# An LSTM step in two halves: two instead of three units of the second half's products ahead of the wait for the second half's h

## The chip, the cores and the metric

The kernel runs on one core of a Trainium2 chip. The time is the device time of one execution in microseconds; the figure for a kernel is the median of several executions. Traces come from one further execution, taken by the hardware profiler.

## What is computed

The input x is 4 sequences of 1024 steps with 512 features. Four layers are applied one after the other, each with a residual: a sparsifying mask, an LSTM, a gated scan, and a second LSTM. The change is in the code of the LSTMs, which run 1024 steps each, 2048 together:

```python
xW = einsum('ntd,dg->ntg', x, Wx) + b
def step(carry, xw_t):
    prev_h, prev_c = carry
    a = xw_t + prev_h @ Wh
    i = sigmoid(a[:, :512]); f = sigmoid(a[:, 512:1024])
    o = sigmoid(a[:, 1024:1536]); g = tanh(a[:, 1536:])
    next_c = f * prev_c + i * g
    next_h = o * tanh(next_c)
    return ((next_h, next_c), next_h)
```

h and c have 4 rows (the batch) of 512 values. Every step needs the h of the step before, so the steps cannot overlap each other.

## The kernel before, in words

`program` (L884) runs five stages in turn: `load_and_sparsify`, `lstm` with names that begin with p_, `gated_scan`, `lstm` with names that begin with q_, and `store`. The LSTM keeps features on the partitions. The 512 hidden values are four chunks k of 128; the 2048 gate columns are split in two **halves** called first (A) and second (B): each half has all four gates of two of the chunks of h. So the first half makes chunks 0 and 1 of the new h, and the second half makes chunks 2 and 3, but both halves need all four chunks of the old h.

**A unit of products** is one call of `h_product` (L406 to L412): the four matmuls j = 0 to 3 of one half, one chunk k of h and one part of the weights. The weights are two float16 parts (high and low), so that a half needs 4 chunks x 2 parts = 8 units a step: 4 with chunks 0 and 1 (`of_first`) and 4 with chunks 2 and 3 (`of_second`). Each of the four matmuls writes its own 32 partitions of the half's PSUM bank (tile PA or PB), with 256 columns; the four run beside each other in the array. h itself (tile H) is stored as a high and a low float16 part.

**The order on PE** (TensorE) is written out by hand in a loop of 128 rounds of 8 steps (v = 0, 1 and u = 0 to 3):

```python
in_between, rest = of_first[:BETWEEN], of_first[BETWEEN:]   # L417
...
pe.wait_ge(s["h_a"], now)                                   # L443
for k, part in of_first:
    h_product(first, v, u, k, part)
for k, part in in_between:
    h_product(second, v, u, k, part)
pe.wait_ge(s["h_b"], now)                                   # L448
for k, part in of_second:
    last = h_product(first, v, u, k, part)
last.then_inc(s["gates_a"], 1)                              # L451
for k, part in rest + of_second:
    last = h_product(second, v, u, k, part)
last.then_inc(s["gates_b"], 1)                              # L454
```

After it come four units of products of x for later steps (L459, matmuls of line L402), and in the steps with u = 0 two bias products (L456 to L458, line L397). So a step is: wait for h_a (chunks 0 and 1 are there), 4 units of A, some units of B, wait for h_b (chunks 2 and 3), 4 units of A, signal gates_a, the remaining units of B, signal gates_b.

**The order on DVE** (VectorE, L626 to L661) is also fixed. Here "first" and "second" are the halves. Wait for gates_a; transpose the first half's gates out of PA (L633, L634, both at line L597); add the two parts of h's products, `both_parts` (L602), signal pre_a; wait for gates_b (L637) and transpose the second half's i, f and g out of PB (L638); wait for g_a and `multiply` the first half (L605); wait for that transpose and run `both_parts` on the second half together with the first's o gate (L642), signal pre_b; `new_c` of the first half (L608); transpose and add the second's o gate; `whole_h`, `high_h` of the first (L615, L618); `multiply` the second; `low_h` of the first (L623), signal h_a; `new_c` of the second; wait for tc_b; `whole_h`, `high_h`, `low_h` of the second, signal h_b.

**ACT** (ScalarE, L494 to L508) answers in between: tanh of the first half's gates (L497, signals g_a), sigmoid of its o (L500), tanh of its c (L502), then the same for the second half (L503, L506, L508). **POOL** (GpSimd, L379 to L389) works every fourth step: it adds h onto x (L389) when the fourth h_b has come, and splits the x of a later group of steps (L355, L356, L359).

Of the kernel before, what the change touches and what calls it, by code (L numbers as in the profile page):

```python
# [31 lines left out]
XCOLS = T * B  # L32
V = 4
VB = V * B
BETWEEN = 3
SUMS = NC * B
PREP = 6
XTAIL = 2 * UB
# [212 lines left out]
def lstm(nc, m, tag, x_all, weights, wh, b, wh_there, also_load=()):  # L251
# [7 lines left out]
    with ExitStack() as ctx:  # L259
# [132 lines left out]
        def _(pe):  # L392
# [23 lines left out]
            of_second = [(k, part) for k in second.ks for part in range(2)]  # L416
            in_between, rest = of_first[:BETWEEN], of_first[BETWEEN:]  # L417

# [504 lines left out]
```

## Time and profile before

| | us |
|---|---|
| median of 3 runs | 7890.69 (7889.62 to 7891.22) |
| the profiled execution, its own time | 7896.71 |
| its span in the trace | 7894.5 |
| PE matmul busy | 5371.6 (68%) |
| DVE busy | 5546.4 (70%) |
| ACT busy | 2263.5 (29%) |
| POOL busy | 843.5 (11%) |

The span is the time from the first to the last instruction of the profiled execution. A busy share is the time in which at least one instruction of the engine was under way. In the rows, "PE" is the matmul side of TensorE and "PEld" its weight loads; L409 is the matmul inside `h_product`. The start times of two instructions on the same engine can be nearer to each other than one lasts, since the engines are pipelined. An entry x16 is sixteen matmuls merged, that is four units.

### The profile page before, as it was taken

What the parts mean: (1) busy time and instruction counts of PE and PEld (TensorE: products, weight loads), DVE (VectorE), ACT (ScalarE), POOL (GpSimd) and SP (SyncE); (2) the same over time, 40 slices, a digit from 0 to 9 for tenths busy, and PEclk for the clock granted to TensorE, in tenths of its full rate; (3) what the DMA queues carried; (4) which work ended last, traced back from release to release, by engine and by line L of the source; (5) the groups of instructions that cost most, each with busy time, mean ns of one, the idle gap of its engine ahead of it and who ended that gap; (6) DMA issues with size and microseconds to landing.
All of it is one profiled execution on the core that took longest, in us unless ns stands there. A gap on an engine that the chain in (4) does not pass through costs nothing. (4 is left out here: it accounts for less than half of the span.)

```text
span 7894.5 us, 402402 instructions
## 1 busy us (share of the span) xinstructions
PE 5371.6 (68%) x169280; PEld 4152.5 (53%) x169280; DVE 5546.4 (70%) x35379; ACT 2263.5 (29%) x12741; POOL 843.5 (11%) x2143
## 2 busy tenths in 40 slices
PE   1577777666777777666983776667777776667776
PEld 0455555555555555555431555555555555555555
DVE  7766777776666677776678777776666777766666
ACT  4322222222222222222354222222222222222222
POOL 5100000000000000000013000000000000000000
PEclk5899999999999999999996999999999999999999
DMA  2000000000000000000001000000000000000001
GB/s 85 17 0 0 0 0 0 0 0 0 0 0 0 0 0 0 0 0 0 0 0 43 0 0 0 0 0 0 0 0 0 0 0 0 0 0 0 0 0 43
DMA packets 32261, 37.24 MB, mean 5 GB/s; under 512 B 6112, under 2 KB 22496, under 8 KB 32224
## 3 DMA queue, kind: packets, MB, share of 16 engines
q1 hardware_dynamic: 32224, 36.76, 1.4%
q8 instruction: 21, 0.34, 0.0%
q14 instruction: 16, 0.13, 0.0%
HBM read 28.34 MB, written 8.39 MB: 5 GB/s over the span
## 5 line engine op out<-in xcount | busy, mean ns | idle before, releaser
L409 PE MATMUL q_PA<-scratch,q_H 128*8 128x256 f16 (+1 forms) x32768 | 1258.3, 274 | 1058.9 <-DVE q_H L623 1058.9
L409 PE MATMUL p_PA<-scratch,p_H 128*8 128x256 f16 (+1 forms) x32768 | 1257.5, 274 | 1059.0 <-DVE p_H L623 1059.0
L409 PEld LDWEIGHTS q_PA<-scratch,q_H 128*8 128x8 f16 (+1 forms) x32768 | 647.8, 90 | 1487.4 <-DVE q_H L623 1346.8
L409 PEld LDWEIGHTS p_PA<-scratch,p_H 128*8 128x8 f16 (+1 forms) x32768 | 647.3, 90 | 1487.4 <-DVE p_H L623 1346.8
L409 PE MATMUL q_PB<-scratch,q_H 128*8 128x256 f16 (+1 forms) x32768 | 1250.1, 273 | 0.0
L409 PE MATMUL p_PB<-scratch,p_H 128*8 128x256 f16 (+1 forms) x32768 | 1249.6, 273 | 0.0
L597 DVE STREAM_TRANSPOSE q_GT<-q_PA 128x192 f32<-128x192 f32 (+1 forms) x2048 | 526.3, 295 | 744.7 <-PE q_PA L409 744.7
L597 DVE STREAM_TRANSPOSE p_GT<-p_PA 128x192 f32<-128x192 f32 (+1 forms) x2048 | 526.3, 295 | 743.8 <-PE p_PA L409 743.8
L409 PEld LDWEIGHTS q_PB<-scratch,q_H 128*8 128x8 f16 (+1 forms) x32768 | 834.7, 92 | 59.9
L409 PEld LDWEIGHTS p_PB<-scratch,p_H 128*8 128x8 f16 (+1 forms) x32768 | 834.1, 92 | 60.2
L497 ACT ACTIVATE q_GBA<-q_PREA 128x24 f32<-128x24 f32 x1024 | 194.8, 190 | 1898.0 <-DVE q_PREA L602 1898.0
L497 ACT ACTIVATE p_GBA<-p_PREA 128x24 f32<-128x24 f32 x1024 | 195.0, 190 | 1896.6 <-DVE p_PREA L602 1896.6
L597 DVE STREAM_TRANSPOSE q_GT<-q_PB 128x192 f32<-128x192 f32 (+1 forms) x2048 | 639.5, 312 | 0.0
L597 DVE STREAM_TRANSPOSE p_GT<-p_PB 128x192 f32<-128x192 f32 (+1 forms) x2048 | 639.4, 312 | 0.0
L389 POOL TENSOR_TENSOR xb<-xb,q_HH 128x64 f32 x256 | 81.9, 320 | 3164.3 <-DVE q_H L623 3164.3
L389 POOL TENSOR_TENSOR xa<-xa,p_HH 128x64 f32 x256 | 81.7, 319 | 3163.7 <-DVE p_H L623 3163.7
L602 DVE TENSOR_TENSOR q_PREA<-q_GT 128x24 f32<-128x24 f32 (+1 forms) x2048 | 368.2, 180 | 34.9
L602 DVE TENSOR_TENSOR p_PREA<-p_GT 128x24 f32<-128x24 f32 (+1 forms) x2048 | 368.0, 180 | 34.9
L738 PE MATMUL g_z<-xa,scratch 128*128 128x512 f32 x768 | 352.2, 620 | 48.2 <-DVE scratch L790 45.6
L623 DVE SCALAR_TENSOR_TENSOR q_H<-q_HH,q_H 128x8 f16<-128x8 f32 x2048 | 342.1, 167 | 35.5
L623 DVE SCALAR_TENSOR_TENSOR p_H<-p_HH,p_H 128x8 f16<-128x8 f32 x2048 | 341.9, 167 | 35.4
L615 DVE TENSOR_TENSOR p_HH<-p_SIGOB,p_TCB 128x8 f32<-128x8 f32 x1024 | 166.2, 162 | 251.9 <-ACT p_TCB L508 251.9
(220 smaller groups left out, 9260.0 us busy)
## 6 DMA issues: line engine op xcount, KB each, us to landing
scratch<-in_x_dram SPq DMA_DIRECT2D x8, 1024.0 KB, 5.4
out_dram<-xa SPq DMA_DIRECT2D x16, 512.0 KB, 6.0
xb<-in_L_cond_Wx_dram SPq DMA_DIRECT2D x8, 384.0 KB, 6.4
xb<-in_L_cond_Wh_dram SPq DMA_DIRECT2D x8, 384.0 KB, 6.2
xa<-in_L_cond_Wx_dram SPq DMA_DIRECT2D x8, 384.0 KB, 5.9
xa<-in_L_cond_Wh_dram SPq DMA_DIRECT2D x8, 384.0 KB, 6.0
xb<-in_L_cond_Wx_dram SPq DMA_DIRECT2D x8, 128.0 KB, 6.7
xb<-in_L_cond_Wh_dram SPq DMA_DIRECT2D x8, 128.0 KB, 6.5
```

The lines of the kernel that those rows point to most:

```text
L389: nc.gpsimd.tensor_tensor(here, here, HH[:, v].rearrange("p u (c b) -> p c u b", b=B), ALU.add).then_inc(s["xadd"], 1)
L409: last = nc.tensor.matmul(half.banks[buf][Q * j:Q * j + rows, 0:GA * Q], H[:, u, k, 0:rows], w16[:, part, k, j, half_cols(half)], start=False,
L497: nc.scalar.activation(first.tanhs, first.pre_gif.rearrange("p (n m) -> p n m", n=3), ACT.Tanh, scale=half_scale).then_inc(s["g_a"], 1)
L597: return nc.vector.transpose(GT[:, lo:hi, :].rearrange("p g n -> p (g n)"), half.banks[v][:, (lo - half.at) * Q:(hi - half.at) * Q])
L602: return nc.vector.tensor_tensor(by_unit(dst), GT[:, lo:hi, at:at + B], GT[:, lo:hi, at + B:at + 2 * B], ALU.add)
L615: return nc.vector.tensor_tensor(HH[:, v, u, half.cols], half.sig_o[:], half.tanh_c, ALU.mult)
L623: return nc.vector.scalar_tensor_tensor(nxt[:, :, B:2 * B], by_unit(HH[:, v, u, half.cols]), H_SCALE, nxt[:, :, 0:B], ALU.mult, ALU.subtract)
L738: last = nc.tensor.matmul(banks[w * 2 + n % 2][:], wt[:, w, k, c * P:(c + 1) * P], m.xa[:, k, blk * TBB:(blk + 1) * TBB], start=(k == 0), ...
```

## The change

The constant `BETWEEN` goes from 3 to 2. With it `in_between` is the first two of `of_first` and `rest` the last two: the unit (k = 1, high part) of the second half's products, four matmuls, is issued behind the wait for h_b and the four units of the first half, instead of ahead of them. The order of the sums within each bank, all instructions and all signals stay.

```diff
 VB = V * B
-BETWEEN = 3
+BETWEEN = 2
 SUMS = NC * B
```

## Rows read from the trace of the kernel before

**Rows 1.** The page: span, engines, a group of weight loads (busy, mean ns, idle)

```profile
span 7894.5 us, 402402 instructions
...
PE 5371.6 (68%) x169280; PEld 4152.5 (53%) x169280; DVE 5546.4 (70%) x35379; ACT 2263.5 (29%) x12741; POOL 843.5 (11%) x2143
...
L409 PEld LDWEIGHTS q_PA<-scratch,q_H 128*8 128x8 f16 (+1 forms) x32768 | 647.8, 90 | 1487.4 <-DVE q_H L623 1346.8
```

**Rows 2.** One stretch: busy PE, PEld, DVE, ACT, POOL, then granted clock, DMA

```profile
400.00:3700.00 3300.00, 2311.37 (x78312) 1841.12 (x78304) 2309.27 (x16235) 874.77 (x5730) 289.77 (x952) 1.00 0.00 0
```

**Rows 3.** Waits, 400 to 3700 us: total us, times, longest us

```profile
PE p_PA L409 <- DVE p_H L623: 988.6, 955, 1.1
DVE p_GT L597 <- PE p_PA L409: 690.3, 955, 0.7
```

**Rows 4.** Timeline of one step: start us, us, engine, line, operation

```profile
2004.55 0.61 PE L409 MATMUL p_PA<-scratch,p_H 128*16 128x256 f16 x16 [0.86 <-DVE p_H L623]
...
2004.99 0.50 PE L409 MATMUL p_PB<-scratch,p_H 128*16 128x256 f16 x12
2005.10 0.17 DVE L623 SCALAR_TENSOR_TENSOR p_H<-p_HH,p_H 128x8 f16<-128x8 f32 x1
...
2005.32 0.61 PE L409 MATMUL p_PA<-scratch,p_H 128*16 128x256 f16 x16
...
2005.76 0.72 PE L409 MATMUL p_PB<-scratch,p_H 128*16 128x256 f16 x20
2005.98 0.51 DVE L597 STREAM_TRANSPOSE p_GT<-p_PA 128x192 f32<-128x192 f32 x2 [0.72 <-PE p_PA L409]
...
2006.30 0.61 PE L402 MATMUL p_PA<-xb,p_XH 128*32 128x256 f16 x16
2006.42 0.17 DVE L602 TENSOR_TENSOR p_PREA<-p_GT 128x24 f32<-128x24 f32 x1
2006.53 0.38 DVE L597 STREAM_TRANSPOSE p_GT<-p_PB 128x192 f32<-128x192 f32 x1
2006.63 0.19 ACT L497 ACTIVATE p_GBA<-p_PREA 128x24 f32<-128x24 f32 x1 [1.83 <-DVE p_PREA L602]
2006.85 0.18 DVE L605 SCALAR_TENSOR_TENSOR p_PRA<-p_GBA 128x16 f32<-128x16 f32 x1
2006.95 0.20 DVE L602 TENSOR_TENSOR p_PREB<-p_GT 128x32 f32<-128x32 f32 x1
...
2007.77 0.17 DVE L623 SCALAR_TENSOR_TENSOR p_H<-p_HH,p_H 128x8 f16<-128x8 f32 x1
...
2007.99 0.62 PE L409 MATMUL p_PA<-scratch,p_H 128*24 128x256 f16 x16 [1.07 <-DVE p_H L623]
```

**Rows 5.** Timeline of the first step of a round

```profile
1905.48 0.72 PE L409 MATMUL p_PB<-scratch,p_H 128*8 128x256 f16 x20
...
1906.05 0.32 POOL L356 TENSOR_TENSOR p_XH<-xa,p_SXB 128x64 f16<-128x64 f32 x1
...
1906.15 0.27 DVE L602 TENSOR_TENSOR p_PREA<-p_GT 128x24 f32<-128x24 f32 x1
...
1906.33 0.37 DVE L597 STREAM_TRANSPOSE p_GT<-p_PB 128x192 f32<-128x192 f32 x1
...
1906.51 0.32 POOL L359 TENSOR_TENSOR p_XH<-p_XC,p_XH 128x64 f16<-128x64 f32 x1
1906.67 0.20 DVE L605 SCALAR_TENSOR_TENSOR p_PRA<-p_GBA 128x16 f32<-128x16 f32 x1
1906.79 0.19 DVE L602 TENSOR_TENSOR p_PREB<-p_GT 128x32 f32<-128x32 f32 x1
```

**Rows 6.** Line L497: duration min/median/max, first and last start

```profile
L497 ACT ACTIVATE p_GBA<-p_PREA x1024: 190/190/193, 247.6 to 3782.9; 128x24 f32<-128x24 f32 x171
```

**Rows 7.** Timeline of PE where the second LSTM's loop begins, at the lower clock

```profile
4325.76 1.09 PE L409 MATMUL q_PA<-scratch,q_H 128*8 128x256 f16 x16
4326.61 0.67 PE L409 MATMUL q_PB<-scratch,q_H 128*8 128x256 f16 x8
```


## The prediction, made before the changed kernel was run

> **What bounds the kernel now.** I read the page first. Neither PE (68% of the span) nor DVE (70%) is full [rows 1], and the split by stages says why: through the LSTM loop PE is busy 2311 of 3300 us and DVE 2309, with TensorE granted its full clock, 2.4 GHz [rows 2]. Two engines at 70% each that take turns are a chain, not a shortage of either. The waits show the turns: in 955 steps PE waits 988.6 us for h from DVE (1.04 a step), and DVE waits 690.3 us for PE's gates (0.72 a step) [rows 3]. DMA is idle there. So the time is the length of one step's chain, 2048 times: 3.44 us a step (2004.55 to 2007.99) [rows 4], or 3.456 as the mean over a whole LSTM, (3782.9 - 247.6) / 1023 [rows 6].
>
> The reader should follow one step in the timeline [rows 4]. PE starts the 4 units of A at 4.55 (leaving out 2000), 3 units of B at 4.99, the other 4 units of A at 5.32, the remaining 5 units of B at 5.76, the products of x at 6.30. From 5.32 to 6.30 nine units go by in 0.98, so **a unit costs 0.109 us**. DVE transposes A at 5.98 and B at 6.53; each starts 0.05 after the last matmul of its half ends (5.32 + 0.61 = 5.93; 5.76 + 0.72 = 6.48). So B's transpose is held by gates_b and by nothing on DVE.
>
> **What sets the second start of A.** The second half's h is written at 5.10 + 0.17 = 5.27, and A's second batch starts 0.05 later, at 5.32. The same 0.05 stands between the first half's h (7.77 + 0.17 = 7.94) and the next first batch (7.99), where PE is certainly waiting [rows 4]. The three units of B also end their issue at 4.99 + 3 x 0.109 = 5.32. Both meet on the same hundredth: three units just fill the wait, and the wait is not shorter than they are.
>
> **The change part by part.** Nothing is removed or added; one unit of B (four matmuls) moves behind the wait and behind the second batch of A. No queue but PE's has another order.
>
> 1. *Ahead of the wait:* PE is through with B at 4.99 + 0.22 = 5.21, and waits till 5.32. Gain: none, since h_b doesn't come sooner. The 0.11 becomes idle PE. Cost of a drained engine at the restart: no row shows this very place drained. One bound is a whole weight load with nothing to hide it, 0.09 us (a mean of 90 ns) [rows 1]; the other is nothing, or 0.01 gained if the queue held it. The nearest row is the first batch, same shapes, after a real wait: 4 units in 4.99 - 4.55 = 0.44, and the second batch takes 5.76 - 5.32 = 0.44 as well [rows 4]. I take 0, with 0.01 either way, and keep the bare load as a rival.
> 2. *A's second batch* starts and ends as before: gates_a and DVE's transposes at 5.98, `both_parts` at 6.42, ACT's tanh at 6.63 don't move.
> 3. *B behind it* is six units, not five: its last matmul ends at 6.59, and DVE's transpose moves from 6.53 to 6.64, **+0.109**. In DVE's fixed queue the first half's `multiply` stands behind this wait, though its own input is there: tanh ends at 6.63 + 0.19 = 6.82, and it starts 0.03 later, at 6.85 [rows 4]. It can't start before the transpose has gone through, at most 0.32 after its start (6.53 to 6.85): 6.96 at the latest. `both_parts` of the second half needs the whole transpose: 6.91 and 0.04 on, 6.95 now; then 7.02 and 0.04 on, 7.06, again +0.11. Slack there is 0.
> 4. *What follows* down to the first half's h (6.95 to 7.77) is DVE back to back with ACT's answers between, each started by these two, so it moves whole. Step: 0.77 (4.55 to 5.32) + 10 units 1.09 + 0.23 (last unit's start plus one to DVE: 6.53 - 6.30) + 1.46 (6.53 to 7.99) = 3.55 against 3.44.
> 5. *Hidden, cost 0:* the products of x start 0.11 later; PE was idle 0.86 to 1.07 before the next h_a, and that h_a is later too. If that cover were gone it would be 0.11 again. POOL and ACT wait for the same h and gates and have no shorter path.
>
> **The first step of a round** (one in eight, 256 in all) is different [rows 5] (times leave out 1900). `both_parts` takes 0.27 there instead of 0.17, and ends at 6.42, 0.05 after POOL's L356 (6.05 + 0.32 = 6.37). So B's transpose starts at 6.33, while PE had it ready for 5.48 + 0.72 + 0.05 = 6.25. A gates_b later by 0.109 gives 6.36: +0.03. `multiply` is then at 6.36 + 0.32 = 6.68 against 6.67, and `both_parts` at 6.36 + 0.37 + 0.04 = 6.77 against 6.79 now, where it stands 0.12 behind the `multiply`. The stall that is paid there today covers nearly all of the unit: 0 to 0.03, I take 0.005; the far bound is the full 0.109.
>
> The row shows that stall; the Trainium skill has a rule for it (page "SBUF — State Buffer", section "Who interferes with whom"): a DVE instruction with two SBUF inputs and a GpSimd one that reads SBUF exclude each other, and the later blocks fully. The trace agrees with it twice, `both_parts` ending 0.05 after L356 and `multiply` (6.67 + 0.20 = 6.87) 0.04 after L359 (6.51 + 0.32 = 6.83). By it the end of this `multiply` is fixed by POOL and the first step would cost 0, not 0.005: a total smaller by 1 us.
>
> **Sum:** 1792 x 0.109 = 195.3, and 256 x 0.005 = 1.3: **+196.6 us**. The profiled execution took 7896.71 (span 7894.5 and 2.2 around it), so it would take 8093.3; the median of the runs is 6.0 below the profiled one, so I forecast 7890.7 + 196.6 = **8087 us**, 2.5% slower. Its own range: the hundredths of the rows are worth 0.005 x 1792 = 9 us either way, 8078 to 8096.
>
> **Rivals.**
> - *The first step pays in full* (slower by more): the stall on POOL moves along with the unit instead of covering it. 2048 x 0.109 = 223 us: 8114. For it: the stall's causes are only seen from outside. Against: both ends at POOL's instruction. 12%.
> - *Part of the unit is absorbed*: DVE finds 0.01 or so (6.82 + 0.03 is what holds `multiply` now, not the transpose). 1792 x 0.096 = 172: 8063. Against it: `both_parts` has no slack. 5%.
> - *Not slower, the other side:* the second batch of A is held by PE's own queue, not by h_b. Then one unit fewer ahead of it starts it 0.11 sooner, at 5.21, gates_a comes 0.11 sooner, gates_b when it does now, and seven steps in eight stay (B's transpose and `both_parts` are held by gates_b); in the first of a round `both_parts` may get ahead of POOL and save up to 0.11: 256 x 0.11 = 28 us. So 7863 to 7891. It decides if h_b is there before 5.32 by more than a hundredth or two. For it: three units end on that same hundredth. Against: the 0.05 after h's write, equal to that of the batch which surely waits. 5% (2 faster by over 0.2%, 3 within). Within it stands the case that the change has no effect since the wait has none.
> - *The restart of the drained engine costs a bare weight load:* 2048 x 0.09 = 184 us more, 8271. Against it the two equal 0.44. 2%.
> - *The clock:* PE's idle time is cut into two pieces a step. Where PE began the second LSTM's loop at half clock, 1.2 GHz, after the idle preparation, four units took 4326.61 - 4325.76 = 0.85, 0.2125 each [rows 7]. If the loop ran so, 16 units in a row would be 3.40 instead of 0.77 + 1.09, +1.54 on 3.55 and 2048 steps: about 11,240 us. Against: the loop already has a pause of about 1 us in each step and was granted the full clock through 3300 us [rows 2]. 1%. The Trainium skill (page "TensorE: Matmul & The Clock Gate", section "A second HAM failure mode: psum-queue depth-cycling") says that frequent short idles between groups of matmuls can make the clock swing between its two levels; the rows with such idles show no swing, and hang no more than this 1% on it.
>
> **How the numbers follow.** Forecast 75%, first step in full 12%, absorbed 5%, not slower 5%, bare load 2%, clock 1%. The range 8063 to 8115 takes in the forecast's own range and the next two cases; what is left out is about 1 in 10. About 0.2%, 16 us, is what a measurement of this kernel can tell from no change. Faster 0.02, same 0.03, slower 0.95.
>
> **What the changed profile would show.** Twelve matmuls between the batches become eight, twenty become twenty-four. A pause of 0.11 before the second batch of A, put down to DVE L623, so PE's waits of that kind double in number. The second batch 0.77 after the first, as now; A's transpose 0.66 after that; B's transpose 0.66 behind A's, now 0.55, and `multiply` 0.32 behind it, with ACT done 0.1 before. Steps of 3.55; in the first of a round a `both_parts` of 0.27 still, and hardly a longer step. L497 spans 1023 x 3.552 = 3634 us in each LSTM. I am wrong if the second batch starts before 0.77, or if `both_parts` follows gates_b by less than now.

## The result and the profile after

The changed kernel takes **8065.75 us** (median, 8062.28 to 8067.49) against 7890.95 for the kernel before (7889.62 to 7895.05): a ratio of 1.0219, with an interval of 1.0206 to 1.0232. That is 175 us slower. The forecast was 8087, 197 us slower, in a range of 8063 to 8115. Its own narrower range, 8078 to 8096, does not hold the result.

The page of the changed kernel, with the span and the engines' busy time:

```profile
span 8060.2 us, 402402 instructions
...
PE 5590.9 (69%) x169280; PEld 4151.8 (52%) x169280; DVE 5635.7 (70%) x35379; ACT 2248.5 (28%) x12741; POOL 846.6 (11%) x2143
```

The number of instructions is the same. The span of this one execution is 165.7 us longer than that of [rows 1]; it lies at the low end of its runs, while the traced execution of before lay above its own. So the traces differ by 166 us and the medians by 175.

One stretch of the first LSTM's loop, as in [rows 2] (PE, PEld, DVE, ACT, POOL, granted clock, DMA):

```profile
400.00:3700.00 3300.00, 2357.80 (x76512) 1798.41 (x76512) 2296.79 (x15862) 847.71 (x5598) 286.28 (x936) 1.00 0.00 0
```

The clock is still granted in full. Fewer instructions go by in the same 3300 us, on every engine. The waits of the same stretch, beside [rows 3]:

```profile
PEld p_PA L409 <- DVE p_H L623: 1408.9, 1866, 1.3
PE p_PA L409 <- DVE p_H L623: 942.4, 933, 1.1
```

There are now 933 steps in the stretch, not 955. PE's weight loads wait for h twice a step (1866 times; once a step, 955 times, before), and its matmuls are still shown as waiting once, since the modelled end of the last matmul of B covers the new gap. Now one step in the timeline, to be laid beside [rows 4]:

```profile
1946.54 0.61 PE L409 MATMUL p_PA<-scratch,p_H 128*16 128x256 f16 x16 [0.86 <-DVE p_H L623]
...
1946.98 0.39 PE L409 MATMUL p_PB<-scratch,p_H 128*16 128x256 f16 x8
1947.09 0.17 DVE L623 SCALAR_TENSOR_TENSOR p_H<-p_HH,p_H 128x8 f16<-128x8 f32 x1
1947.31 0.33 PEld L409 LDWEIGHTS p_PA<-scratch,p_H 128*16 128x16 f16 x16 [0.22 <-DVE p_H L623]
1947.31 0.61 PE L409 MATMUL p_PA<-scratch,p_H 128*16 128x256 f16 x16
...
1947.75 0.83 PE L409 MATMUL p_PB<-scratch,p_H 128*16 128x256 f16 x24
1947.97 0.51 DVE L597 STREAM_TRANSPOSE p_GT<-p_PA 128x192 f32<-128x192 f32 x2 [0.72 <-PE p_PA L409]
...
1948.62 0.19 ACT L497 ACTIVATE p_GBA<-p_PREA 128x24 f32<-128x24 f32 x1 [1.83 <-DVE p_PREA L602]
1948.63 0.38 DVE L597 STREAM_TRANSPOSE p_GT<-p_PB 128x192 f32<-128x192 f32 x1
1948.94 0.13 DVE L605 SCALAR_TENSOR_TENSOR p_PRA<-p_GBA 128x16 f32<-128x16 f32 x1
1949.05 0.20 DVE L602 TENSOR_TENSOR p_PREB<-p_GT 128x32 f32<-128x32 f32 x1
1949.16 0.16 DVE L608 SCALAR_TENSOR_TENSOR p_GBA<-p_PRA 128x8 f32<-128x8 f32 x1
1949.23 0.24 DVE L597 STREAM_TRANSPOSE p_GT<-p_PB 128x64 f32<-128x64 f32 x1
...
1949.86 0.17 DVE L623 SCALAR_TENSOR_TENSOR p_H<-p_HH,p_H 128x8 f16<-128x8 f32 x1
...
1950.08 0.62 PE L409 MATMUL p_PA<-scratch,p_H 128*24 128x256 f16 x16 [1.06 <-DVE p_H L623]
```

With times that leave out 1900: A's first batch 46.54, two units of B at 46.98 (x8), and a weight load that waited 0.22 for DVE L623. The second batch starts at 47.31, 0.77 after the first and 0.05 after the second half's h (47.09 + 0.17), exactly as before. Six units of B (x24) follow it. A's transpose is at 47.97, 0.66 behind the batch as before; ACT's tanh too is where it was, 0.65 behind the transpose. But B's transpose stands 0.66 behind A's, not 0.55, and `multiply` at 48.94, when its input has been there since 48.62 + 0.19 = 48.81. From 46.54 to 50.08 the step takes 3.54, not 3.44.

Behind `both_parts` the two kernels also differ. In the step of [rows 4], `both_parts` (6.95) is followed by:

```profile
2007.06 0.17 DVE L608 SCALAR_TENSOR_TENSOR p_GBA<-p_PRA 128x8 f32<-128x8 f32 x1
2007.14 0.24 DVE L597 STREAM_TRANSPOSE p_GT<-p_PB 128x64 f32<-128x64 f32 x1
```

From `new_c` to the transpose behind it, it was 0.08 before (7.06 to 7.14) and is 0.07 after (49.16 to 49.23).

The first step of a round, beside [rows 5]:

```profile
1944.43 0.52 DVE L597 STREAM_TRANSPOSE p_GT<-p_PA 128x192 f32<-128x192 f32 x2 [0.72 <-PE p_PA L409]
...
1944.76 0.32 POOL L356 TENSOR_TENSOR p_XH<-xa,p_SXB 128x64 f16<-128x64 f32 x1
...
1944.86 0.26 DVE L602 TENSOR_TENSOR p_PREA<-p_GT 128x24 f32<-128x24 f32 x1
...
1945.08 0.38 DVE L597 STREAM_TRANSPOSE p_GT<-p_PB 128x192 f32<-128x192 f32 x1
...
1945.39 0.20 DVE L605 SCALAR_TENSOR_TENSOR p_PRA<-p_GBA 128x16 f32<-128x16 f32 x1
1945.51 0.19 DVE L602 TENSOR_TENSOR p_PREB<-p_GT 128x32 f32<-128x32 f32 x1
1945.62 0.17 DVE L608 SCALAR_TENSOR_TENSOR p_GBA<-p_PRA 128x8 f32<-128x8 f32 x1
1945.70 0.24 DVE L597 STREAM_TRANSPOSE p_GT<-p_PB 128x64 f32<-128x64 f32 x1
```

`both_parts` (44.86) is as long as before and ends at 45.12, 0.04 after POOL's L356. B's transpose starts at 45.08, 0.65 behind A's (44.43), but `multiply` (45.39) comes 0.63 behind POOL's L356 and 0.12 ahead of the second `both_parts` (45.51), against 0.62 and 0.12 before. This step got no longer. Over a whole LSTM, as in [rows 6]:

```profile
L497 ACT ACTIVATE p_GBA<-p_PREA x1024: 191/191/193, 247.3 to 3865.8; 128x24 f32<-128x24 f32 x171
```

(3865.8 - 247.3) / 1023 = 3.537 us a step, 0.081 more than 3.456; times 2048 that is the 166 us.

### The profile page after: what moved, and what is told of

It is laid out like the page before. It is cut to its first block and busy times, and to the rows that moved or that the text cites. A ratio compares the mean times of both kernels' runs of the same rounds, so it can differ in the third digit from the quotient of the medians.

```text
span 8060.2 us, 402402 instructions
## 1 busy us (share of the span) xinstructions
PE 5590.9 (69%) x169280; PEld 4151.8 (52%) x169280; DVE 5635.7 (70%) x35379; ACT 2248.5 (28%) x12741; POOL 846.6 (11%) x2143
## 5 line engine op out<-in xcount | busy, mean ns | idle before, releaser
L497 ACT ACTIVATE q_GBA<-q_PREA 128x24 f32<-128x24 f32 x1024 | 196.2, 192 | 1895.7 <-DVE q_PREA L602 1895.7
L497 ACT ACTIVATE p_GBA<-p_PREA 128x24 f32<-128x24 f32 x1024 | 196.2, 192 | 1894.1 <-DVE p_PREA L602 1894.1
L623 DVE SCALAR_TENSOR_TENSOR q_H<-q_HH,q_H 128x8 f16<-128x8 f32 x2048 | 341.4, 167 | 35.4
L623 DVE SCALAR_TENSOR_TENSOR p_H<-p_HH,p_H 128x8 f16<-128x8 f32 x2048 | 341.3, 167 | 35.4
L615 DVE TENSOR_TENSOR q_HH<-q_SIGOB,q_TCB 128x8 f32<-128x8 f32 x1024 | 166.4, 162 | 251.6 <-ACT q_TCB L508 251.6
```

Source lines behind the costliest of these rows:

```text
L497: nc.scalar.activation(first.tanhs, first.pre_gif.rearrange("p (n m) -> p n m", n=3), ACT.Tanh, scale=half_scale).then_inc(s["g_a"], 1)
L615: return nc.vector.tensor_tensor(HH[:, v, u, half.cols], half.sig_o[:], half.tanh_c, ALU.mult)
L623: return nc.vector.scalar_tensor_tensor(nxt[:, :, B:2 * B], by_unit(HH[:, v, u, half.cols]), H_SCALE, nxt[:, :, 0:B], ALU.mult, ALU.subtract)
```

## The experiments

All times are medians; the kernel before was run beside each group (7886.2 us for the first four, 7898.9 for the two with POOL, 7898.0 for the last two), so I quote the difference to that. Where differences of two groups are compared, a few us mean nothing.

**One: the moved unit is left out.** The sixth unit behind the wait isn't computed, and PE runs dry ahead of the wait all the same:

```diff
-BETWEEN = 3
+BETWEEN = 2
-                        for k, part in rest + of_second:
+                        for k, part in rest[1:] + of_second:
```

> Two units of B ahead of the wait, and the third one left out altogether: five units of B stand behind A's second batch, as in the kernel before, and PE still runs dry ahead of it (the second half's gates lack the product of chunk 1 with the high part of the weights). Theory (the whole cost is the sixth unit in front of gates_b): B's transpose 0.55 us behind A's, a step of 3.44 us, 7891 us. Rival (restarting a drained PE, or the longer idle time, costs by itself): some of the 175 us stays, 7920 to 8066 us.

Measured: 7884.2 us, ratio 0.9998 (0.9989 to 1.0008). In its timeline:

```profile
1905.73 0.33 PEld L409 LDWEIGHTS p_PA<-scratch,p_H 128*16 128x16 f16 x16 [0.22 <-DVE p_H L623]
1905.73 0.61 PE L409 MATMUL p_PA<-scratch,p_H 128*16 128x256 f16 x16
...
1906.17 0.72 PE L409 MATMUL p_PB<-scratch,p_H 128*16 128x256 f16 x20
1906.40 0.51 DVE L597 STREAM_TRANSPOSE p_GT<-p_PA 128x192 f32<-128x192 f32 x2 [0.72 <-PE p_PA L409]
...
1906.94 0.38 DVE L597 STREAM_TRANSPOSE p_GT<-p_PB 128x192 f32<-128x192 f32 x1
```

PE waits 0.22 ahead of the second batch, restarts at once, and with five units behind it B's transpose is 0.54 behind A's. All of the cost is the unit's place in front of gates_b. An idle and restarted PE costs nothing that the runs can tell: the interval is 9 us under to 6 us over.

**Two: one unit more behind the wait.**

```diff
-BETWEEN = 3
+BETWEEN = 1
```

> BETWEEN = 1: one more unit moves behind the wait. Theory: the 14 ns a step that were saved against the forecast come once, as the instructions of DVE behind the transpose stop being held by a signal that arrives just in time; the first step of a round has used up its cover too. So the second unit costs its full 0.109 us in all 2048 steps: 223 us on 8066, 8289 us. Rival (each unit costs about 95 ns in seven steps of eight): 2048 x 0.095 = 195 or less, 8261 us or below.

Measured: 8280.9 us, ratio 1.0500 (1.0483 to 1.0518), 394.7 us over before. The first moved unit cost 174.8, so the second cost about 220 us, 0.107 us in each of 2048 steps. The theory's 223 is near, the rival's 195 is not.

```profile
1999.82 0.33 PEld L409 LDWEIGHTS p_PA<-scratch,p_H 128*16 128x16 f16 x16 [0.33 <-DVE p_H L623]
...
2000.26 0.94 PE L409 MATMUL p_PB<-scratch,p_H 128*16 128x256 f16 x28
2000.48 0.51 DVE L597 STREAM_TRANSPOSE p_GT<-p_PA 128x192 f32<-128x192 f32 x2 [0.72 <-PE p_PA L409]
...
2001.25 0.38 DVE L597 STREAM_TRANSPOSE p_GT<-p_PB 128x192 f32<-128x192 f32 x1 [0.15 <-PE p_PB L409]
```

The wait ahead of the second batch is 0.33, seven units (x28) stand behind, and B's transpose is 0.77 behind A's: again one unit, 0.11. So the first unit was cheaper than the second, for two reasons: the first step of a round absorbs little more than one, and some ten nanoseconds are saved once. By the traces, with two and with one unit, the second unit lengthens seven steps of eight by its whole 0.109 (3.535 to 3.644) and the first of a round by 0.092 (3.552 to 3.644). That makes 219 us; the 223 of the expectation took 0.109 for all steps.

**Three: four units ahead of the wait.**

```diff
-BETWEEN = 3
+BETWEEN = 4
```

> BETWEEN = 4: all of the units with chunks 0 and 1 ahead of the wait. Theory: h_b is there at 0.77 us after the first batch, PE reaches the wait only at 0.88, so A's second batch, A's transpose, the tanh and the multiply move by 0.109 us while gates_b stays; multiply and both_parts follow the tanh, so a step grows by 0.10 to 0.11 us in seven of eight, and in the first of a round POOL's instruction covers it: 1792 x 0.109 = 195, 8086 us. Rival (only gates_b sets the time): 7891 us. Second rival (the second batch was held by PE's queue, not by h_b): the same as the theory here, but then BETWEEN = 2 would have moved the second batch forward.

Measured: 8082.0 us, ratio 1.0250 (1.0232 to 1.0267), 195.8 over before, as the theory had it.

```profile
1951.54 0.61 PE L409 MATMUL p_PB<-scratch,p_H 128*16 128x256 f16 x16
...
1951.98 0.61 PE L409 MATMUL p_PA<-scratch,p_H 128*16 128x256 f16 x16
...
1952.64 0.51 DVE L597 STREAM_TRANSPOSE p_GT<-p_PA 128x192 f32<-128x192 f32 x2 [0.83 <-PE p_PA L409]
...
1953.16 0.38 DVE L597 STREAM_TRANSPOSE p_GT<-p_PB 128x192 f32<-128x192 f32 x1
1953.29 0.19 ACT L497 ACTIVATE p_GBA<-p_PREA 128x24 f32<-128x24 f32 x1 [1.94 <-DVE p_PREA L602]
1953.51 0.18 DVE L605 SCALAR_TENSOR_TENSOR p_PRA<-p_GBA 128x16 f32<-128x16 f32 x1
```

Here the sixteen matmuls of B run past the moment when h_b is there. The second batch starts 0.44 after B, with no wait, and the tanh is late in the place of B's transpose: `multiply` starts at 53.51, 0.03 after the tanh ends (53.29 + 0.19), although B's transpose starts early (0.52 behind A's). With two units gates_b holds the step, with four gates_a does. Three is where both meet.

**Four: the gap is filled.** One unit of the products of x runs in the gap, in the steps with u = 1 to 3:

```diff
-BETWEEN = 3
+BETWEEN = 2
...
                             h_product(second, v, u, k, part)
+                        if u:
+                            x_product(x_order[4 * u][0], 1 - v, *x_order[4 * u][1:])
                         pe.wait_ge(s["h_b"], now)
...
-                        for half, k, part in x_order[4 * u:4 * u + 4]:
+                        for half, k, part in x_order[4 * u + (u > 0):4 * u + 4]:
```

> BETWEEN = 2, and in the steps with u = 1 to 3 one unit of the products of x in the gap ahead of the wait, taken from the four behind gates_b. Theory: the gap is idle time that nothing needs and the x products have cover behind; no change against two units, 8066 us, and the second batch still starts 0.77 us after the first. Rival (a PE that restarts dry is slower, or a filled one is): some ns a step either way, above 8 us in all.

Measured: 8062.5 us, ratio 1.0224 (1.0207 to 1.0241), 176.3 over before; the change alone has 174.8.

```profile
1947.03 0.61 PE L409 MATMUL p_PA<-scratch,p_H 128*16 128x256 f16 x16 [0.86 <-DVE p_H L625]
...
1947.47 0.39 PE L409 MATMUL p_PB<-scratch,p_H 128*16 128x256 f16 x8
...
1947.69 0.28 PE L402 MATMUL p_PA<-xb,p_XH 128*32 128x256 f16 x4
...
1947.80 0.61 PE L409 MATMUL p_PA<-scratch,p_H 128*16 128x256 f16 x16
```

The unit of x sits at 47.69 in what was the gap, and the second batch starts at 47.80, 0.77 after the first, as with the gap. Work in the gap is free, but this work was free behind gates_b too. Only a unit that stands in front of gates_b gains from being there.

**Five and six: POOL taken out of the first step of a round.** POOL's loop is cut at another place: it splits the x of a later group right behind the adding of h, so that its jump back falls in its long wait.

```diff
+            pool.wait_ge(s["xw"], 1)
+            pool.wait_ge(s["xh"], 2)
+            parts_of_x(xt_ahead[:, :, 0:VB], 0, 3)
             with pool.Fori(0, ROUNDS) as r:
                 for v in range(2):
-                    done = pool.snap(r * 2 + (v + 1))
-                    pool.wait_ge(s["xw"], done)
-                    pool.wait_ge(s["xh"], pool.snap(r * 2 + (v + 2)))
-                    parts_of_x(xt_ahead[:, :, bass.ds(r * UB + v * VB, VB)], v, pool.snap(r * 2 + (v + 3)))
...
+                    pool.wait_ge(s["xw"], pool.snap(r * 2 + (v + 2)))
+                    pool.wait_ge(s["xh"], pool.snap(r * 2 + (v + 3)))
+                    parts_of_x(xt_next[:, :, bass.ds(r * UB + v * VB, VB)], 1 - v, pool.snap(r * 2 + (v + 4)))
```

(`xt_next` is a view of x one group of four steps further on than `xt_ahead`.) Five has it with three units ahead of the wait, six with two.

> BETWEEN = 3 as before, POOL's loop cut elsewhere: the x of a later group is split behind the adding of h, so that POOL's jump falls in its long wait and its two instructions L355 and L356 come some 0.25 us sooner in the first step of a round, as they do in the fifth. Theory: both_parts there takes 0.17 us, the first step loses the 0.113 us by which it is longer (3.554 against 3.441 us): 256 x 0.113 = 29 us, 7862 us. Rival (the loop's jump on DVE or ACT makes that step long): 7891 us.

> BETWEEN = 2 with the same cut of POOL's loop. Theory (in the first step of a round POOL's stall and the later gates_b lie beside each other, so that each hides the other): taking the stall away gives hardly anything, 256 x 0.01 = 3 us, 8063 us, and the cost of the moved unit without POOL in the way is 8063 - 7862 = 201 us. Rival (the stall and the later gates add up): 29 us less here too, 8037 us.

Measured: with three units 7871.4 us, ratio 0.9966 (0.9952 to 0.9979), 27.5 us under before; with two 8069.5 us, ratio 1.0217 (1.0203 to 1.0231), 170.7 over before. `both_parts` of the kernel before, and then of number five, where the line is L605 (duration min/median/max in ns):

```profile
L602 DVE TENSOR_TENSOR p_PREA<-p_GT x2048: 170/175/274, 247.4 to 3783.7; 128x24 f32<-128x24 f32 x94, 128x8 f32<-128x8 f32 x93
```

```profile
L605 DVE TENSOR_TENSOR p_PREA<-p_GT x2048: 170/174/176, 248.2 to 3770.0; 128x24 f32<-128x24 f32 x94, 128x8 f32<-128x8 f32 x93
```

The long ones, up to 274, are gone. Both rivals are out: the jumps of the loops of DVE and ACT are where they were, and the gain of 27.5 us does not come a second time with two units. Without POOL in the way three units gain 27.5 us and two gain only 174.8 - 170.7 = 4 (their first step of a round is 0.014 shorter in the trace, 256 x 0.014 = 3.6): what the stall costs and what the later gates_b costs lie beside each other in that step, and only the longer one counts. And between these two kernels the moved unit costs 170.7 + 27.5 = 198 us, 0.097 us in every one of 2048 steps. Number five is faster than both kernels of this case.

**Seven and eight: a part of the unit.** Of the unit behind the wait only 64 or 128 of its 256 columns are computed:

```diff
-BETWEEN = 3
+BETWEEN = 2
...
-                        for k, part in rest + of_second:
+                        h_product(second, v, u, *rest[0], cols=64)
+                        for k, part in rest[1:] + of_second:
```

(128 in number eight; `h_product` gets the argument `cols` for the width of its output and weights.)

> BETWEEN = 2, and of the unit that moves behind the wait only 64 of its 256 columns are computed (three quarters of one product of the second half are left out), so gates_b comes about 0.027 us later than before, not 0.109. Theory (the saving of 14 ns a step comes as soon as new_c is no longer held by a multiply that ends just in time): a step grows by 0.027 - 0.014 = 0.013 us in seven of eight, 1792 x 0.013 = 23 us over before, ratio 1.003. Rival (the saving is in proportion to the delay, 95 ns for 109): 0.024 us a step, 43 us, ratio 1.0054. Third (a slack of 13 ns ahead of multiply that is filled first): 23 us too, but with an unchanged start of both_parts.

> The same with 128 of 256 columns (half of the product left out): gates_b about 0.054 us later than before. Theory: 0.054 - 0.014 = 0.040 us in seven steps of eight, 72 us over before, ratio 1.0091. Rival (in proportion): 0.047 us, 85 us, ratio 1.0107.

Measured: 7933.5 us with 64 columns, ratio 1.0044 (1.0030 to 1.0058), 35.5 over before; 7979.2 us with 128, ratio 1.0102 (1.0086 to 1.0118), 81.2 over before. Both intervals hold both expectations, so the times don't decide. The traces do. B's transpose came 0.029 and 0.056 later than before, and a step that is not the first of a round grew by 0.019 (3.4415 to 3.4609) and 0.046 (to 3.4872): 0.010 less, both times. In proportion to the delay it would be 0.004 and 0.007 less. `new_c` of the first half (L608, in seven and eight L609), duration min/median/max in ns, in the kernels before, after and seven:

```profile
L608 DVE SCALAR_TENSOR_TENSOR p_GBA<-p_PRA x1024: 165/167/168, 248.1 to 3783.3; 128x8 f32<-128x8 f32 x171
```

```profile
L608 DVE SCALAR_TENSOR_TENSOR p_GBA<-p_PRA x1024: 156/159/168, 247.9 to 3866.3; 128x8 f32<-128x8 f32 x171
```

```profile
L609 DVE SCALAR_TENSOR_TENSOR p_GBA<-p_PRA x1024: 158/159/168, 249.5 to 3802.2; 128x8 f32<-128x8 f32 x171
```

Before, its median is 167; as soon as gates_b is late at all, even by a quarter of a unit, it is 159 (in number eight too). The next instruction of DVE then starts 0.077 behind it, not 0.084. Another 0.003 are saved just ahead of `new_c`. Before, it starts 0.034 behind the end of the `multiply` (7.03 to 7.06), whose result it needs, and 0.112 behind `both_parts`; with gates_b late the `multiply` ends long before it, and it starts 0.109 behind `both_parts`. That is 0.010 us saved once, whatever the delay: (0.029 - 0.010) x 1792 = 34 us for a quarter of a unit and (0.056 - 0.010) x 1792 = 82 for half, beside 35.5 and 81.2 measured.

The third case of the expectation, a slack ahead of the `multiply` that is filled first, with `both_parts` where it was, is out. In number seven:

```profile
1918.84 0.51 DVE L598 STREAM_TRANSPOSE p_GT<-p_PA 128x192 f32<-128x192 f32 x2 [0.72 <-PE p_PA L409]
...
1919.41 0.38 DVE L598 STREAM_TRANSPOSE p_GT<-p_PB 128x192 f32<-128x192 f32 x1
...
1919.83 0.20 DVE L603 TENSOR_TENSOR p_PREB<-p_GT 128x32 f32<-128x32 f32 x1
```

`both_parts` is 0.99 behind A's transpose, 0.97 before, and 0.42 behind B's, as before.

My 14 ns in the expectations was 4 too many. I had it from one trace of each kernel, and these two lie on different sides of their medians: before's took 7896.7 us (median 7891.0), after's 8062.3 (median 8065.8). Together that is 9 us, 4 to 5 ns a step. Between numbers five and six, which ran beside each other, such a step grows by 0.098 to 0.099 in the traces, and by 0.098 between numbers one (3.436) and four (3.534).

## Why the prediction was right, and what it mis-sized

**The bound and the second start of A: right.** The second batch waits for h_b: its start stayed at 0.77 behind the first with two units (47.31), with one, and with the gap filled (0.766 to 0.771 in the medians over each trace), and it moved only with four, when PE itself came late. The rival in which PE's queue held it, so that the change would not be slower, is out: gates_a came no sooner.

**The restart of the drained engine, costed at 0: right.** The batch's four units take 0.44 after the gap (47.31 to 47.75), and number one shows no cost of the gap in the time. In the medians over 700 steps of each trace the batch takes 0.443 after the gap and 0.439 without it, and starts 0.054 behind h's write, not 0.057: two effects of a few nanoseconds that nearly cancel. The rival of a bare weight load is out.

**Six units instead of five, +0.109 on gates_b: right.** B's transpose is 0.66 behind A's.

**"It moves whole" (part 4): the term that was too large.** I had 0.109 in seven steps of eight; number six less number five gives 0.097 over all steps, and their traces 0.098 to 0.099 in those seven. The delay reaches `both_parts` whole (1.08 behind A's transpose, 0.97 before), and then shrinks. I read the spacing of DVE's instructions in the trace before as fixed; but the `multiply` and `new_c` were held there by a signal that came just in time (both start 0.03 behind the end of what they wait for), and with the gates late their inputs are there ahead. The trace shows that with the durations of the `multiply`, before and after:

```profile
L605 DVE SCALAR_TENSOR_TENSOR p_PRA<-p_GBA x1024: 174/176/200, 247.8 to 3783.1; 128x16 f32<-128x16 f32 x171
```

```profile
L605 DVE SCALAR_TENSOR_TENSOR p_PRA<-p_GBA x1024: 130/132/201, 247.6 to 3866.1; 128x16 f32<-128x16 f32 x171
```

It shrinks from 176 to 132 ns, and `new_c` by 8. The first brings nothing by itself, since `new_c` then follows `both_parts`. What counts is that `new_c` no longer waits for the `multiply` (0.003) and that the instruction behind the shorter `new_c` starts sooner (0.007). 0.010 x 1792 = 18 us of the 22 between 197 and 175; the rest is less than the interval of the measurement.

That being held goes with the longer `new_c` is what all ten kernels agree in: the median is 159 in those with two units or fewer ahead of the wait (left-out columns too), 166 or 167 in those with three or four and in number one, where gates_b is not late. The changed kernel shows it by itself too. In its first step of a round, where the `multiply` is long (45.39 + 0.20 = 45.59), `new_c` starts 0.03 behind it (45.62), takes 0.17, and the transpose follows 0.08 behind; in its other steps `new_c` is not held, takes 0.16, and 0.07 follows. Why a held instruction is recorded longer is open, and the hold was not changed alone.

**The first step of a round at nothing: right**, and shown from both sides by numbers five and six. The rival in which it pays in full, 8114, is out. The Trainium skill's rule (page "SBUF — State Buffer", section "Who interferes with whom"), that a DVE instruction with two SBUF inputs and a GpSimd one that reads SBUF exclude each other, fits: with POOL's instructions moved away, the stall of 0.1 is gone (`both_parts` 176 at most, not 274).

**Part of the unit absorbed, 8063, at 5%:** this is the case that came nearest, and by luck. Its size is nearly the measured one (172 us for 175), its place is not: no slack ahead of `multiply` was used up; an earlier and shorter `new_c` behind it did it. The stated range reached down to 8063 only because of this case, and so it holds 8065.75 by less than 3 us, while the forecast's own range ends at 8078. The mechanism and the path were right; that the result lies inside the range is partly luck.

**The clock: right.** It was granted at 1.00 with a second idle piece in each step. The Trainium skill's case of short idles that make it swing (page "TensorE: Matmul & The Clock Gate", section "A second HAM failure mode: psum-queue depth-cycling") doesn't occur here.

## What to carry to other kernels

Where an engine fills a wait with work that another engine needs soon after, the right amount is what ends just when the wait does: one unit less or one more both cost nearly a unit in seven steps of eight here, by two different signals. To see which, compare the start behind the wait with the time of the signal and not with the work ahead of it. And before a delay is added to every step, look for the steps in which another stall already covers it.

## What was not expected of the hardware

The recorded length of a short DVE instruction goes with whether its input came just in time or was there: 176 against 132 ns for a `multiply` of 128x16, 167 against 159 for a `new_c` of 128x8, each with the same operands. It is not a matter of yes or no. In number seven the `multiply` starts 0.05 behind the end of the tanh, not 0.03, and takes 161 in the median.

A chain of such instructions read from a trace is therefore a little longer than the same chain when something ahead of it is late, here by 0.010 in a step of 3.44.
